# Attention over pooled cells: scores with the cells on partitions, and the normalisation moved behind the projection

## The reference, cut to what matters

```python
# x: (8, 512, 64, 64) f32; qk_w (256, 512), v_w (512, 512), out_w (512, 512)
qk  = relu(bn(conv1x1(x, qk_w)))                 # (8, 256, 64, 64)
val = relu(bn(conv1x1(x, v_w)))                  # (8, 512, 64, 64)
key   = psp(qk)                                  # adaptive max pooling to 1+9+36+64 = 110 cells
value = psp(val).transpose(0, 2, 1)              # (8, 110, 512)
scores = einsum('bnc,bcs->bns', query, key) * 256 ** -0.5      # query is qk, one row per pixel
scores = softmax(scores, axis=-1)                # over the 110 cells
y = einsum('bns,bsc->bnc', scores, value)        # (8, 4096, 512)
y = bn(conv1x1(y, out_w))
return x + y
```

## Time and profile before

| | us |
|---|---|
| median of three timed runs | 1456.84 (1455.62 to 1458.07) |
| span of the profiled execution, first to last instruction | 1453.4 |
| PE busy | 1421.5 (98% of the span) |
| PEld busy | 1170.7 (81%) |
| DVE busy | 927.5 (64%) |
| ACT busy | 368.2 (25%) |
| POOL busy | 0.7 |
| mean granted TensorE clock | 0.995 of full speed |
| DMA of a tile, issue to landing: load of 1024 KB, store of 1024 KB | 5.5, 4.2 (medians) |

### The profile page before, as it was taken

How to read it: one execution, slowest core, us unless ns; L and a number is a source line. 1 busy time by engine, 2 the same in 40 slices (tenths; PEclk the granted TensorE clock), 3 DMA queues, 4 the chain that set the end, 5 groups by cost and what they waited for, 6 DMA issues and landing times.

```text
span 1453.4 us, 19136 instructions
## 1 busy us (share of the span) xinstructions
PE 1421.5 (98%) x6761; PEld 1170.7 (81%) x6761; DVE 927.5 (64%) x1736; ACT 368.2 (25%) x917; POOL 0.7 (0%) x6
## 2 busy tenths in 40 slices
PE   7999999999999999999999999999999999999998
PEld 6888788887788877888778887788877888788876
DVE  5655666675656756667566675666756667666668
ACT  3112232232221322312213223132231322322222
POOL 0000000000000000000000000000000000000000
PEclk9999999999999999999999999999999999999999
DMA  5211032232222322322323223132231322322116
GB/s 189 86 59 58 30 116 91 84 117 87 89 97 78 116 88 88 116 83 92 103 74 116 87 88 114 62 116 88 87 117 59 116 88 87 117 87 87 59 60 230
DMA packets 69176, 138.24 MB, mean 95 GB/s; under 512 B 2218, under 2 KB 2258, under 8 KB 69074
## 3 DMA queue, kind: packets, MB, share of 16 engines
q1 hardware_dynamic: 68498, 135.82, 27.1%
q10 hardware_dynamic: 576, 1.05, 0.2%
HBM read 69.75 MB, written 67.11 MB: 94 GB/s over the span
## 4 chain that ended last, share of the span: by engine, by line
PE 96%; issue 1%; DVE 1%; ACT 0%; DMA 0%; DVEq 0%; SPq 0%
PE conv_ps L284 24%; PE conv_ps L285 24%; PE conv_ps L286 24%; PE score_ps L324 7%; PE out_ps L309 4%; PE out_ps L311 4%; PE out_ps L310 4%; PE t_ps L332 2%; PE t_ps L297 2%; PE conv_ps L324 0%; DVE pt_l L597 0%; DVE row_max L544 0%; DMA xr<-x 0%; ACT q L423 0%; PE conv_ps L311 0%
## 5 line engine op out<-in xcount | busy, mean ns | idle before, releaser
L544 DVE TENSOR_REDUCE row_max<-conv_ps 128x64 f32<-128x384 f32 (+2 forms) x384 | 193.4, 532 | 240.2 <-PE conv_ps L286 234.6
L284 PE MATMUL conv_ps<-xh_a,wh 128*128 128x512 f32 x768 | 316.3, 412 | 0.0
L285 PE MATMUL conv_ps<-xh_a,wl 128*128 128x512 f32 x768 | 303.8, 396 | 0.0
L286 PE MATMUL conv_ps<-xl_a,wh 128*128 128x512 f32 x768 | 303.0, 395 | 0.0
L284 PE MATMUL conv_ps<-xh_b,wh 128*128 128x512 f32 x768 | 301.0, 392 | 0.0
L285 PE MATMUL conv_ps<-xh_b,wl 128*128 128x512 f32 x768 | 299.9, 390 | 0.0
L286 PE MATMUL conv_ps<-xl_b,wh 128*128 128x512 f32 x768 | 299.6, 390 | 0.0
L436 ACT ACTIVATE probs<-score_ps,neg_max 128x110 f32<-128x110 f32 x240 | 81.5, 352 | 846.5 <-DVE neg_max L603 846.5
L544 DVE TENSOR_REDUCE row_max<-q 128x64 f32<-128x512 f32 (+2 forms) x192 | 142.4, 769 | 87.6 <-ACT q L423 87.6
L592 DVE SCALAR_TENSOR_TENSOR xr<-out_ps,shift,xr 128x512 f32 (+1 forms) x238 | 177.5, 748 | 9.0 <-PE out_ps L311 1.4
L286 PEld LDWEIGHTS conv_ps<-xl_a,wh 128*128 128x128 f32 x768 | 145.5, 189 | 33.4
(11 more groups left out here) (75 smaller groups left out, 1012.3 us busy)
## 6 DMA issues: line engine op xcount, KB each, us to landing
xr<-x SPq DMA_DIRECT2D x63, 1024.0 KB, 5.5
out<-xr SPq DMA_DIRECT2D x63, 1024.0 KB, 4.2
q<-v_w ACTq DMA_DIRECT2D x4, 256.0 KB, 4.5
xr<-x SPq DMA_DIRECT2D x2, 512.0 KB, 5.7
q<-out_w SPq DMA_DIRECT2D x1, 1024.0 KB, 7.8
out<-xr SPq DMA_DIRECT2D x4, 256.0 KB, 2.1
q<-qk_w SPq DMA_DIRECT2D x1, 512.0 KB, 7.6
bn_rows<-bn_params SPq DMA_DIRECT2D x1, 20.0 KB
```

The lines of the kernel that those rows point to most:

```text
L284: nc.tensor.matmul(bank[:, :], wh[:, k, cols], hi, start=(n == 0), stop=False)
L285: nc.tensor.matmul(bank[:, :], wl[:, k, cols], hi, start=False, stop=False)
L286: last = nc.tensor.matmul(bank[:, :], wh[:, k, cols], lo, start=False, stop=(n == KC - 1))
L544: last = nc.vector.tensor_reduce(row_max[:, c, n, :], src[:, r0 * W:r1 * W].rearrange("p (r w) -> p w r", w=W), AX.X, ALU.max)
```

## The change

The scores come out with the cells on partitions: `key_h`, `key_l` are the stationary side and the split `q_h`, `q_l` the moving one, six fp32r matmuls of 512 columns. The first cell's key is subtracted from all keys, so that no maximum is taken, and the exponential of a tile is one ACT instruction on 110 x 512. There is nothing to transpose. Split into `e_h` and `e_l`, the unnormalised exponentials go into `project`. A product with a matrix of ones gives every partition the 512 sums (`sums`), DVE inverts them in one instruction on 128 x 512 (`invert`), and DVE multiplies each output chunk with the result into `y` (`scale_out`). GpSimd adds x (`add_residual`), which is loaded a second time into `xo`; x for the convolution lies in `xa`, two tiles. The shift of the output's batch norm is added to `vo` once for an image. `q` is pooled out of PSUM before batch norm's shift and relu, which `finish_grids` applies to the cells. `value` times out_w is 12 fp32r matmuls instead of 4 fp32 ones.

```diff
             def step(b, t):
+                if scored(b):
+                    if not isinstance(b, int) or NT * b + t >= NT + 2:
+                        stored(*((b, t - 1) if t >= 1 else (b - 1, NT - 1)))
+                    load_residual(b, t)
                 if not isinstance(b, int) or NT * b + t + 2 < NT * B:
...
+                    wait(sp, x_lo, b, t, 2, 2)
+                    load(b, t + 2)
+                if projected(b, t):
...
+            def add_residual(b, t, m):
+                tt = (t - 1) % NT
+                bb = b - 1 if t >= 1 else b - 2
+                if m == 0:
+                    pool.wait_ge(xo_in[tt], (bb + 1) * 16)
+                wait(pool, out_scaled, b, t, OC, m + 1 - (NT + 1) * OC)
+                xt = xo[:, tt % 2, m, :]
+                nc.gpsimd.tensor_tensor(xt, y[:, m % 2, :], xt, ALU.add).then_inc(out_added, 1)
...
+            def turn_shift():
+                pe.wait_ge(shift_spread, 1)
+                pe.wait_ge(w_lo, PAR - 1)
+                for m in range(OC):
+                    last = nc.tensor.transpose(setup_ps[0][0:CELLS, m * P:(m + 1) * P], shift_rows[:, m, :], ident[:, :])
+                last.then_inc(shift_turned, 1)
...
+            def sums(b, t):
+                wait(pe, e_lo, b, t, 1, 1 - (NT + 1))
                 if t == 1:
+                    pe.wait_ge(vo_made, b)
+                wait(pe, rsum_ready, b, t, 1, (-1 if sum_bank(b, t) is conv_ps[1] else 0) - (NT + 1))
+                u = (t - 1) % 2
+                nc.tensor.matmul(sum_bank(b, t)[:, :], ones[:, :], e_h[:, u, :], start=True, stop=False)
+                nc.tensor.matmul(sum_bank(b, t)[:, :], ones[:, :], e_l[:, u, :], start=False, stop=True)\
+                    .then_inc(sums_done, 1)
+            def project(b, t, m):
+                if m == 0 and t == 1:
                     pe.wait_ge(vo_lo, b)
...
                 four = isinstance(b, int) and NT * b + t > NT * B
                 if m < 2 or four or not (isinstance(b, int) and b >= B):
...
+                    wait(pe, out_scaled, b, t, OC, m - (3 if four else 1) - (NT + 1) * OC)
+                cols, u = slice(m * P, (m + 1) * P), (t - 1) % 2
+                bk = out_bank(b, t, m)
+                nc.tensor.matmul(bk[:, :], vo_h[:, cols], e_h[:, u, :], start=True, stop=False)
+                nc.tensor.matmul(bk[:, :], vo_l[:, cols], e_h[:, u, :], start=False, stop=False)
+                nc.tensor.matmul(bk[:, :], vo_h[:, cols], e_l[:, u, :], start=False, stop=True).then_inc(out_done, 1)
             def scores(b, t):
                 if t == 0:
                     pe.wait_ge(key_ready, b)
...
+                wait(pe, q_lo, b, t, 1, 1 - NT)
                 two = isinstance(b, int) and NT * b + t > NT * B
                 wait(pe, exp_done, b, t, 1, -NT - two)
...
+                bk = score_bank(b, t)
+                for i in range(QC):
+                    nc.tensor.matmul(bk[0:CELLS, :], key_h[:, i, :], q_h[:, t % 2, i, :], start=(i == 0), stop=False)
+                    nc.tensor.matmul(bk[0:CELLS, :], key_l[:, i, :], q_h[:, t % 2, i, :], start=False, stop=False)
+                    last = nc.tensor.matmul(bk[0:CELLS, :], key_h[:, i, :], q_l[:, t % 2, i, :], start=False,
+                                            stop=(i == QC - 1))
                 last.then_inc(scores_done, 1)
             def project_values(b):
                 pe.wait_ge(value_ready, b)
...
             def exps(b, t):
...
+                wait(act, scores_done, b, t, 1, 1 - NT)
+                wait(act, e_lo, b, t, 1, -1 - NT)
+                nc.scalar.activation(e[:, t % 2, :], score_bank(b, t)[0:CELLS, :], ACT.Exp).then_inc(exp_done, 1)
+                wait(act, exp_done, b, t, 1, 1 - NT)
+                wait(act, out_done, b, t, OC, -OC * (NT + 1))
+                nc.scalar.activation(e_h[:, t % 2, :], e[:, t % 2, :], ACT.Copy).then_inc(e_hi, 1)
...
+                nc.vector.tensor_scalar(key[:, 0, :], cells[:, VC, :], shift[:, VC:VC + 1], 0.0, ALU.add, ALU.max)
+                grid_chain(nc.vector.tensor_scalar(key[:, 1, :], cells[:, VC + 1, :], shift[:, VC + 1:CC], 0.0,
+                                                   ALU.add, ALU.max))
+                nc.vector.tensor_scalar(key_d[:, 0, :], key[:, 0, :], key[:, 0, 0:1], float(CK) ** -0.5,
+                                        ALU.subtract, ALU.mult)
+                grid_chain(nc.vector.tensor_scalar(key_d[:, 1, :], key[:, 1, :], key[:, 1, 0:1], float(CK) ** -0.5,
+                                                   ALU.subtract, ALU.mult))
+                grid_chain(nc.vector.tensor_copy(key_h[:, :, :], key_d[:, :, :]))
+                nc.vector.tensor_tensor(key_l[:, :, :], key_d[:, :, :], key_h[:, :, :], ALU.subtract).then_inc(key_ready, 1)
                 for m in range(VC):
                     last = nc.vector.tensor_scalar(value[:, m, :], cells[:, m, :], shift[:, m:m + 1], 0.0, ALU.add, ALU.max)
...
+                grid_chain(last)
+                grid_chain(nc.vector.tensor_copy(value_h[:, :, :], value[:, :, :]))
+                nc.vector.tensor_tensor(value_l[:, :, :], value[:, :, :], value_h[:, :, :], ALU.subtract)\
+                    .then_inc(value_ready, 1)
...
+            def invert(b, t):
+                wait(dve, sums_done, b, t, 1, 1 - (NT + 1))
+                wait(dve, out_scaled, b, t, OC, -(NT + 1) * OC)
+                nc.vector.reciprocal(rsum[:, :], sum_bank(b, t)[:, :]).then_inc(rsum_ready, 1)
+                wait(dve, rsum_ready, b, t, 1, 1 - (NT + 1))
+            def scale_out(b, t, m):
                 wait(dve, out_done, b, t, OC, m + 1 - (NT + 1) * OC)
...
+                wait(dve, out_added, b, t, OC, m - 1 - (NT + 1) * OC)
+                nc.vector.tensor_tensor(y[:, m % 2, :], out_bank(b, t, m)[:, :], rsum[:, :], ALU.mult)\
+                    .then_inc(out_scaled, 1)
+            def split_e_lo(b, t):
+                wait(dve, e_hi, b, t, 1, 1 - NT)
+                nc.vector.tensor_tensor(e_l[:, t % 2, :], e[:, t % 2, :], e_h[:, t % 2, :], ALU.subtract).then_inc(e_lo, 1)
+            def split_q_lo(b, t):
+                wait(dve, q_hi, b, t, 1, 1 - NT)
+                nc.vector.tensor_tensor(q_l[:, t % 2, :, :], q[:, t, :, :], q_h[:, t % 2, :, :], ALU.subtract)\
+                    .then_inc(q_lo, 1)
...
+                if has_out:
+                    invert(b, t)
                 for c in range(VC):
                     pool_rows(b, t, c)
                     if has_out:
...
+                        scale_out(b, t, c)
+                    if c in (1, 2) and has_split:
+                        split_lo(*next_tile(b, t), c - 1)
                 if isinstance(b, int) and NT * b + t == 0:
                     for j in range(CC, PAR):
                         scale_weights(j)
+                    spread_shift()
                 if scored(b):
...
+                    split_e_lo(b, t)
                     if t == 0:
+                        make_values(b)
                         values_lo(b)
...
+                if splits_q(b, t):
+                    split_q_lo(*next_tile(b, t))
                 pool_rows(b, t, VC)
...
             def tail():
...
                 pool_cells(B - 1, NT - 1)
                 finish_grids(B)
+                invert(B, 0)
                 for m in range(OC):
...
+                    scale_out(B, 0, m)
+                split_q_lo(B, 1)
+                split_e_lo(B, 0)
+                make_values(B)
                 values_lo(B)
+                split_e_lo(B, 1)
                 for t in range(1, NT + 1):
...
                     if t + 1 < NT:
...
+                        split_q_lo(B, t + 1)
+                    invert(B, t)
                     for m in range(OC):
...
+                        scale_out(B, t, m)
+                    if t + 1 < NT:
+                        split_e_lo(B, t + 1)
```

More of the change, by code:

```diff
@@ L75, in psp_attention @@
         key = sb("key", [P, QC, CELLS])
+        key_d = sb("key_d", [P, QC, CELLS])
+        key_h = sb("key_h", [P, QC, CELLS], F32R)
+        key_l = sb("key_l", [P, QC, CELLS], F32R)
         value = sb("value", [P, VC, CELLS])
+        value_h = sb("value_h", [P, VC, CELLS], F32R)
+        value_l = sb("value_l", [P, VC, CELLS], F32R)
+        shift_rows = sb("shift_rows", [P, OC, CELLS])
+        shift_bc = sb("shift_bc", [CELLS, CIN])
+        vo = sb("vo", [CELLS, CIN])
         vo_h = sb("vo_h", [CELLS, CIN], F32R)
         vo_l = sb("vo_l", [CELLS, CIN], F32R)
-        neg_max = sb("neg_max", [P, 2, SUB])
-        sums = sb("sums", [P, 2, SUB])
-        rsum = sb("rsum", [P, 2, SUB])
-        probs = sb("probs", [P, 2, SUB, CELLS])
-        pt_h = sb("pt_h", [CELLS, TN], F32R)
-        pt_l = sb("pt_l", [CELLS, TN], F32R)
+        q_h = sb("q_h", [P, 2, QC, TN], F32R)
+        q_l = sb("q_l", [P, 2, QC, TN], F32R)
+        e = sb("e", [CELLS, 2, TN])
+        e_h = sb("e_h", [CELLS, 2, TN], F32R)
+        e_l = sb("e_l", [CELLS, 2, TN], F32R)
```

(21 more changed lines are left out.)

342 lines of the change are left out of this document (144 added, 198 removed).

## The result

The changed kernel takes 1495.32 us, median of four runs (1494.45 to 1496.05), against 1456.23 (1454.21 to 1458.07) for the kernel before on the same chip: ratio 1.027, 95% interval 1.0256 to 1.0284. So it is slower by 39 us, inside the predicted range of 1480 to 1548 and 10 us under the forecast of 1505. The profiled execution has a span of 1493.9 us, 40.5 more than before. One of the ten executions of experiment 2 was slow, 1577.57 us at a mean granted clock of 0.84, and no reading rests on it.

What follows compares the result with a forecast made beforehand. PE, busy 98% of the span, was taken as the bound until its convolutions end, then the last engine. -26.1 + 28.2 + 0 + 2.0 + 43.7 = +47.8 us on 1453.4 gave span 1501.2, so 1505 us timed; range 1480 to 1548.

Steps and rivals of the forecast that it cites:

- PE's work: PE's steps with attention before the tail: cheaper scores and values times weights, sums slightly dearer; -26.1 us together.
- The reciprocal: DVE's one instruction on 128 x 512 sums: taken as 4.3 us, bounds 2.6 to 4.6.
- First steps: First step of an image: PE waits 3.0 us for DVE, plus 1.7 of clock, six times; +28.2 us.
- R: The time of DVE's reciprocal on 128 x 512, taken as 4.3 us; it stands 20 times in the sum.
- Loop's returns: Where the loop goes round, five times: PE waits 2.2 us for DVE, as long as before; 0 us.
- Setup: Before the loop: PE turns the shift behind the ninth weight block's low part; +2.0 us.
- The tail: Nine outputs behind the convolutions, bound by DVE with period 9.9 us: 101.0 us against 57.3, so +43.7.
- P: The time of one GpSimd addition of x, taken as 1.2 us; four in a step stop nobody.
- rival 1: GpSimd's additions hold up DVE's differences: usual steps 22.0 us instead of 21.2, 1549 us in all; chance 0.17.
- rival 2: DVE's wide reciprocal costs only 0.7 us, so the kernel gets faster: 1425 us; chance 0.04.
- rival 3: Still slower, all prices low: reciprocal 3.6 us, addition 0.8, no clock lost at new waits; 1473 us; chance 0.08.
- the step from span to timed median: Added to the profiled span of the whole kernel to get the timed median: 3.4 us.

Runs made afterwards that it cites:

- experiment 2: Changed kernel with DVE's wide reciprocal and first product moved ahead of `pool_cells` and `finish_grids`: 1458.19 us, ratio 1.0018 to the kernel before.
- experiment 1: Changed kernel with a copy in place of the wide reciprocal, so the output is left undivided: 1442.08 us, ratio 0.9909 to the kernel before.
- experiment 4: Changed kernel with both loads of x on SP waiting until two convolution chunks of the step are done: 1467.08 us, ratio 1.008 to the kernel before.
- experiment 5: Kernel before, with SP's loop written out and its one load of a step waiting for two convolution chunks: 1440.05 us, ratio 0.9894.
- experiment 8: Changed kernel with 1/sum made on ScalarE as Ln, then Exp with scale -1, instead of DVE's reciprocal: 1439.69 us, ratio 0.9894 to the kernel before.

## Why the prediction was right

- **PE's work**: right. The step is 21.06, forecast 21.54 - 0.38 = 21.16; by the distances between PE's starts the scores save 0.31, the matmuls with ones cost 0.12 more than the transposes did, and the 72 of the convolution, which I left as they were, take 16.38 us where they took 16.67. An fp32r matmul over 110 partitions goes at the rate of its columns, as assumed.
- **The reciprocal**: the mis-sized term. 4.3 taken, 3.35 measured. The slope between 4 and 10 elements gave 3.6 and was the better reading; my argument that a start hides part of it, which moved me to the upper end, failed. The price is 3347 / 512 = 6.5 ns an element, or 6.2 once the first 4 elements' 178 ns are taken off (3169 / 508). The Trainium skill (VectorE: DVE Perf Modes, First, the fixed hardware budget) has a repeat count of 8, by which the estimate was 4.4 us; the trace disagrees, and at that page's 0.96 GHz the measured slope is 6 cycles.
- **First steps**: right in place and mechanism. The wait of 2.1 us instead of 3.0 is R's 0.95; the clock's 1.7 (by the steps themselves 3.94 - 2.36 = 1.6) came in five of six. Experiments 1 and 2 each take the term away.
- **Loop's returns**: the step of the prediction that failed. It said "PE ... waits 2.2 us, as long as before: 0". With R = 3.35 by its own path the wait would have been 1.2; it was 4.07. I took DVE's 3.41 us of return as a constant of the loop, though it grows with the DMA load, and the change doubles the loads of x: 5.45 us, 2.0 more. I also gave PE 0.8 us of return of its own; in the kernel before most of it stood in front of the transposes (PE idle for 0.53 us there, at 725.44), and the changed kernel's trace has no such gap. 1.2, 2.0 and 0.8 make up the 4.07. Experiments 4 and 5 show it from both kernels. The error of only +7.0 in the account hides a large one: the returns cost 30 us in the changed kernel, and 24 of them go with one wait on SP.
- **Setup**: +0.8 instead of +2.0.
- **The tail**: right in size and cause. Period 9.57, forecast 9.9; with R corrected the forecast's would have been 8.95, and `e_l` (+0.4) and the products' waits (4.07 against 3.7) make up the rest. P = 1.2 was the right choice for an addition alone (1.3 on the record); the mean of 1725 ns comes from those that meet DVE's differences and take 2.2 to 2.9. That I called the turn of x's buffers harmless was right for this kernel and wrong for every faster one.
- **Rivals**: 1 fell (usual steps are 21.06, under its 22.0), though its collisions exist: in the tail they cost DVE 0.4 us a tile, and in a usual step it is GpSimd that is held up (108 of 220 additions take 2.2 us or more), where nobody waits for it. 2 and 3 fell with R = 3.35 and P = 1.22.

Several errors of opposite sign made the total better than its parts, and that was luck: against the forecast of +47.8 PE's work is 4.1 less, the first steps 6.1, the setup 1.2, the tail 2.5 and the last step 0.4, while the returns are 7.0 more. The remaining 2 us of the 10 are the step from span to timed median, for which I took 3.4 and which is 1.4 here.

## What to carry to other kernels

Price an operation that only occurs small by its slope between two sizes, and leave the slope only for a reason that a row shows. Where an engine comes back late from a loop, look at the DMA share of that stretch before taking the delay as fixed; loads moved out of it were worth 15 us in one kernel and 28 in the other, 24 of these at the returns. An engine with time to spare on average can still be late at the one place that another waits for, so what the other engine waits for goes to the front of the queue, as in experiment 2, or the long instruction goes to an engine that has the time, as in experiment 8.
